# Weight jobs 14 steps later, tiles 8 to 11 closer, part of the first group's maxima by way of ScalarE

## The chip, the cores and the metric

The kernel runs on one core of one Trainium2 chip. The metric is device time in microseconds; a run ends when the output is written. Engines are named PE (TensorE, matmuls), DVE (VectorE), ACT (ScalarE), POOL (GpSimd) and SP (SyncE, which here only issues DMAs).

## The reference, cut to what is computed

x is 4 x 512 x 512, the context 4 x 1601 x 512, 16 heads of 32 columns; keys and values are both the context as it is. The hidden width of the gated block is 1408.

```python
x = x + tanh(g_xattn[0]) * mha(layernorm(x), ctx, ctx)
x = x + tanh(g_ffn[0]) * ffn(layernorm(x), w_gate, w_up, w_down, ...)
...
scores = einsum('bhqd,bhkd->bhqk', qh, kh) / sqrt(hd)
scores = where(ki <= qi + (Sk - Sq), scores, -10000.0)
out = softmax(scores) @ vh
...
qx, sx, sc = reorder_quantize(x, up_reorder_index)    # rows scaled, rounded to fp8
g, u = qlinear(qx, w_gate), qlinear(qx, w_up)          # weight rows quantized too
t = silu(g) * u
y = qlinear(reorder_quantize(t, down_reorder_index), w_down)
```

## The kernel before

**Attention.** The work is cut into 16 groups (`GALL`) of one batch and four heads. A group has 26 steps (`STEPS`): two head pairs times 13 key tiles of 128 (the last has 65). In a step PE makes the scores of two heads against one key tile (`scores`, L842 and the mask at L848), ACT takes the exponential (`exps`, L632), and PE, two steps later, multiplies by the values (`values`, L866). A score needs the stacked keys and queries `kst`, `qst`, which are 12 DMA copies for each head pair of a group (`put_heads`, L335 and L336), and a row of shifts, the negated maximum of each query, which is one DMA copy of `mrow` (`put_shift`, L340).

**Maxima.** For the shift, PE makes the same products once more from f16 halves (`max_turn`, L780, mask L785), and DVE reduces them out of PSUM (`max_reduce`, L1069). A group has 26 such chunks, two heads times up to 512 keys each; 18 of the 26 are full, and 16 of these have no mask and lie in the first 1024 keys. `max_finish` (L1076 to L1080) joins them, `shift_turn` (L794) transposes, ACT copies to `mrow` (L608). Products and reductions alternate between two slots of PSUM (`numbered`, `free_slot`). In the loop one chunk is done in a step, six steps (`AHEAD`) ahead of its group.

**Order before the loop.** PE, DVE and ACT do: the gates (L928), the stage of group 0 (transposes of keys and x, L767 and L759, split into f16 high and low parts, L592 and L1060), its 26 maxima, the shift, the stage of group 1, and six maxima of group 1. SP issues x, the keys of groups 0 and 1, three value tiles (`load_values`, L321), the 24 head copies of group 0, ten value tiles, the shift row of group 0, two blocks of w_down, the keys of group 2 and the heads of group 1.

**Feed-forward.** 26 weight jobs quantize and turn the weights: jobs 0 to 3 are blocks of w_down (128 x 1408, seven steps apart), 4 to 25 are gathered rows of w_gate and w_up (128 x 512, three steps apart). A job takes its scale on DVE (L999), is scaled by ACT (L562), rounded on DVE (L981, L985, L989), subtracted on POOL (`weight_quant`, L416, semaphore `wq_ready`) and transposed on PE (`weight_turn`, L920). With base b, a w_down job adds on DVE in step b+4, subtracts on POOL in step b+5, and turns on PE in step b+6. Then 16 tiles of 128 rows go through the block, each a chain of 27 steps over all engines (rows turn L874 at 5, up turns L887 at 7, 9, 11 and 13, hidden turn L898 at 23, down turn L910 at 25). Tiles 12 to 15 run after the last scores, which are step 415.

**What sets the order.** Every engine has one program, written step by step, and does it strictly in that order; semaphores tie the engines together. SP's program has no steps: it is one list for each group, and an issue that waits holds back all behind it. The lines of it that matter, at group 0 of the loop (`load_down(sp, o)` waits for `wq_ready` of o - 1 for o >= 2):

```python
                if gg == 0:
                    load_down(sp, 2)
                    load_down(sp, 3)
...
                if gg + 3 < GALL:
                    load_keys(sp, gg + 3)
...
                    put_heads(sp, gg + 2, 0)
...
                    put_shift(sp, gg + 1)
```

Of the kernel before, what the change touches and what calls it, by code (L numbers as in the profile page):

```python
# [5 lines left out]
def flamingo_gated_block(nc, x_d, ctx_d, gx_d, gf_d, wg_d, wu_d, wd_d, didx_d, out_d):  # L6
    nc.disable_value_cache = True
    f32, f16, bf16, i32 = mybir.dt.float32, mybir.dt.float16, mybir.dt.bfloat16, mybir.dt.int32
    ALU = mybir.AluOpType
# [51 lines left out]
    CH = len(chunks)  # L61
    assert CH == STEPS
# [3 lines left out]
    def max_job_at(at):  # L66

        gg, j = divmod(at + AHEAD, STEPS)
        return (gg + 1, j) if gg + 1 < GALL else None
# [12 lines left out]
    def tile_base(n):  # L82

        return STEPS * (n + NG) + 15 if n < TAIL else LAST + 7 + 13 * (n - TAIL)
# [18 lines left out]
    def weight_base(j):  # L103
        return 1 + 7 * j if j < DC else 1 + 7 * DC + 3 * (j - DC)
# [11 lines left out]
    banks, before_in_bank, latest, dve_count, act_count = {}, {}, {}, {}, {}  # L116

    def numbered(*job):
# [13 lines left out]
    for j in range(CH):  # L132
        numbered("max", 0, j)
# [3 lines left out]
    for j in range(AHEAD):  # L137
        numbered("max", 1, j)
    for at in range(END):
# [7 lines left out]
        if max_job_at(at) is not None:  # L147
            numbered("max", *max_job_at(at))
# [15 lines left out]
    with ExitStack() as ctx:  # L164
# [67 lines left out]

        def tile_set(n):
# [47 lines left out]
        mx_mm, m_ready, mT_mm = sem("mx_mm"), sem("m_ready"), sem("mT_mm")  # L281
        mrow_in = [sem("mrow_in0"), sem("mrow_in1")]
# [65 lines left out]
        def _(sp):  # L348
# [6 lines left out]
            for t in range(3):  # L355
# [4 lines left out]
            for t in range(3, NT):  # L360
                load_values(sp, 0, t)
# [131 lines left out]
        def _(pool):  # L493
# [91 lines left out]
        def stage_high(act, gg, part):  # L585
# [6 lines left out]
            nc.scalar.copy(to[:, gg % 2, c0:c1], slot(("stage", gg, part))[:, 0:c1 - c0]).then_inc(hi_done, 1)  # L592

# [96 lines left out]
        def _(act):  # L690
            act.wait_ge(consts, 15)
            act.wait_ge(gate_mm, 1)
            nc.scalar.activation(tg[:, :], ps[:, 0, 0:2], ACT.Tanh).then_inc(gate_th, 1)
# [3 lines left out]
            stage_high(act, 0, 0)  # L697
            norm_cols(act, 1, range(QT))
# [71 lines left out]
        def max_turn(pe, gg, j):  # L770
# [3 lines left out]
            if j == 0:  # L774
# [12 lines left out]
            last.then_inc(mx_mm, 1)  # L787

# [490 lines left out]
```

## Time and profile before

| | us |
|---|---|
| median of three runs | 1158.43 (1156.97 to 1160.3) |
| the profiled execution | 1161.19, its span 1159.4 |
| PE, DVE busy | 970.5 (84%), 859.7 (74%) |
| ACT, POOL busy | 656.5 (57%), 332.1 (29%) |
| mean granted clock of PE | 0.949 of full speed |

The durations that follow come from the one profiled execution, whose times count from the start of its span. A line of the timeline gives start, duration, engine, source line, operation, the tensors written and read, how many instructions are merged, and in brackets how long the engine had been idle and what released it. PEld is PE's weight load, SPq is SP issuing a DMA. The granted clock is a share of 2.4 GHz.

### The profile page before, as it was taken

To read this page: it belongs to the slowest core of one execution; us is meant where nothing else is said; L and a number is where in the kernel's file an instruction comes from. 1 tells how busy PE (TensorE), PEld (TensorE's weight loads), DVE (VectorE), ACT (ScalarE), POOL (GpSimd) and SP (SyncE) were. 2 spreads that over 40 slices of the span, in tenths; PEclk is the share of its full clock that TensorE was granted. 3 is DMA by queue.
4 is the path that set the end of the run, shared out by engine and by line. 5 is a ranking of instruction groups with operands and counts; after the bars stand their busy time and mean duration, and the time that the engine had idled before them with its cause. 6 is when DMAs were issued, how large, how long until landed. Compare 5 with 4: busy or idle time off the path is not lost.

```text
span 1159.4 us, 21085 instructions
## 1 busy us (share of the span) xinstructions
PE 970.5 (84%) x7770; PEld 399.4 (34%) x7770; DVE 859.7 (74%) x1438; ACT 656.5 (57%) x1343; POOL 332.1 (29%) x350
## 2 busy tenths in 40 slices
PE   4588889888879989999889999998899999984344
PEld 2233333333323334343334333333333343432222
DVE  7768789887747888777677877787778786446764
ACT  2165567675646666666556666665566666753321
POOL 3012323332101414132323232222314132443343
PEclk9998899999989999999999999999999999996766
DMA  7942423230572221114812121218421110000000
GB/s 147 154 122 69 115 66 93 66 86 26 112 88 57 66 57 39 53 43 83 124 41 60 63 61 36 51 41 115 70 61 35 27 41 10 2 10 10 10 10 19
DMA packets 155119, 70.69 MB, mean 61 GB/s; under 512 B 111032, under 2 KB 142856, under 8 KB 155016
## 3 DMA queue, kind: packets, MB, share of 16 engines
q1 hardware_dynamic: 153256, 63.57, 26.5%
q0 software_dynamic: 1760, 5.77, 1.8%
q8 instruction: 62, 1.02, 0.4%
q14 instruction: 41, 0.34, 0.1%
HBM read 39.08 MB, written 4.19 MB: 37 GB/s over the span
## 4 chain that ended last, share of the span: by engine, by line
PE 42%; DVE 36%; issue 10%; ACT 4%; POOL 4%; DMA 2%; SPq 1%; POOLq 0%; DVEq 0%; ACTq 0%
DVE mch L1069 17%; PE ps L866 13%; PE ps L842 8%; PE ps L887 6%; PE ps L780 5%; PE ps L910 3%; DVE ff L985 2%; DVE ff L981 2%; DVE ff L989 2%; PE ps L785 2%; ACT pr L632 1%; DVE upd L1112 1%; DMA qst<-mrow 1%; PE ps L848 1%; DVE cmb L1102 1%
## 5 line engine op out<-in xcount | busy, mean ns | idle before, releaser
L632 ACT ACTIVATE pr<-ps 128x512 f32<-128x512 f32 (+4 forms) x832 | 397.2, 530 | 250.0 <-PE ps L842 125.1
L1069 DVE TENSOR_REDUCE mch<-ps 128x2 f32<-128x1024 f32 (+4 forms) x416 | 432.3, 1056 | 69.2 <-PE ps L780 32.8
L866 PE MATMUL ps<-pr,vf 128*33 128x512 f32 (+4 forms) x1664 | 380.6, 537 | 0.0
L842 PE MATMUL ps<-qst,kst 97*64 97x512 f16 (+4 forms) x1600 | 250.5, 371 | 18.0 <-DMA qst<-mrow 11.4
L780 PE MATMUL ps<-kTh,qTh 32*128 32x512 f16 (+4 forms) x832 | 156.2, 373 | 59.2 <-DVE mch L1069 40.7
L780 PEld LDWEIGHTS ps<-kTh,qTh 32*128 32x128 f16 x832 | 39.5, 92 | 279.0 <-DVE mch L1069 106.9
L842 PEld LDWEIGHTS ps<-qst,kst 97*64 97x64 f16 (+1 forms) x1600 | 77.3, 111 | 108.0 <-ACT pr L632 57.4
L866 PEld LDWEIGHTS ps<-pr,vf 128*33 128x33 f32 (+1 forms) x1664 | 86.8, 113 | 56.6 <-issue 4.9
L1141 DVE SCALAR_TENSOR_TENSOR ff<-ps,scs,wsb 128x352 f32<-128x352 f32 x56 | 32.6, 583 | 73.1 <-PE ps L887 73.1
L448 POOL TENSOR_TENSOR t_q<-ff 128x768 bf16<-128x768 f32 (+1 forms) x28 | 47.4, 1694 | 100.1 <-DVE ff L989 100.1
L887 PE MATMUL ps<-wgu,t_T 128*64 128x352 bf16 x768 | 66.5, 316 | 0.0
L429 POOL TENSOR_TENSOR ff<-ff,wsb 128x352 f32<-128x352 f32 x48 | 46.0, 957 | 64.0 <-DVE ff L1141 64.0
L1060 DVE TENSOR_TENSOR kTl<-ps,kTh 128x1024 f16<-128x1024 f32 (+1 forms) x32 | 31.7, 992 | 41.0 <-ACT kTh L592 40.8
L848 PE MATMUL ps<-maskT,idb 128*64 128x128 bf16 (+2 forms) x576 | 61.7, 214 | 0.0
L989 DVE TENSOR_TENSOR ff<-ff 128x512 f32<-128x512 f32 (+3 forms) x66 | 55.0, 833 | 2.1
L659 ACT ACTIVATE ff<-ps,scs 128x352 f32<-128x352 f32 x48 | 26.6, 554 | 52.2 <-PE ps L887 52.2
L453 POOL TENSOR_TENSOR xs<-xs,ff 128x512 f32<-128x512 f32 x14 | 17.8, 1273 | 132.1 <-DVE ff L1179 132.1
L887 PEld LDWEIGHTS ps<-wgu,t_T 128*64 128x64 bf16 x768 | 44.3, 111 | 32.6 <-issue 20.8
L460 POOL TENSOR_TENSOR xs<-xs,upd 128x256 f32<-128x256 f32 x32 | 24.0, 749 | 107.9 <-DVE upd L1112 107.9
L433 POOL TENSOR_TENSOR ff<-ff 128x352 f32<-128x352 f32 x48 | 51.7, 1078 | 3.8
L489 POOL TENSOR_TENSOR cw<-w,count 128x16 f32<-128x16 f32 x16 | 3.9, 245 | 165.9 <-ACT w L615 165.9
L785 PE MATMUL ps<-idb,maskT 128*64 128x128 bf16 (+2 forms) x640 | 47.1, 229 | 0.0
(151 smaller groups left out, 1198.2 us busy)
## 6 DMA issues: line engine op xcount, KB each, us to landing
kst<-kTh SPq DMA_DIRECT2D x128, 100.1 KB, 2.2
ksrc<-in_ctx SPq DMA_DIRECT2D x16, 768.0 KB
vf<-in_ctx SPq DMA_DIRECT2D x48, 256.0 KB, 5.1
kst<-kTl SPq DMA_DIRECT2D x64, 100.1 KB, 2.2
xs<-in_x SPq DMA_DIRECT2D x16, 256.0 KB, 4.8
qst<-qTh SPq DMA_DIRECT2D x128, 32.0 KB, 1.9
out<-xs SPq DMA_DIRECT2D x16, 256.0 KB, 2.0
ff<-in_L_ffn_w_down SPq DMA_DIRECT2D x4, 704.0 KB, 4.4
```

The lines of the kernel that those rows point to most:

```text
L429: nc.gpsimd.tensor_tensor(t_u[e][:, cols], t_u[e][:, cols], wsb[:, I + c * CW:I + (c + 1) * CW], ALU.mult).then_inc(gated, 1)
L433: nc.gpsimd.tensor_tensor(t_u[e][:, cols], t_u[e][:, cols], t_g[e][:, cols], ALU.mult).then_inc(gu_ready, 1)
L448: nc.gpsimd.tensor_tensor(t_q[e][:, cols], t_v[e][:, cols], t_m[e][:, cols], ALU.subtract).then_inc(qt_ready, 1)
L632: nc.scalar.activation(pr[0:kn, n % NP, q0:S], ps[0:kn, j, q0:S], ACT.Exp, scale=SCALE).then_inc(ex_done, 1)
L780: last = nc.tensor.matmul(slot(job)[:, 512 * i:512 * i + k1 - k0], qTh[rows, gg % 2, qt * P:(qt + 1) * P], kTh[rows, gg % 2, k0:k1], start ...
L785: last = nc.tensor.matmul(slot(job)[a:e, 512 * i + lo - k0:512 * i + hi - k0], maskT[:, a:e], idb[:, lo - d0:hi - d0], start=False, stop=True)
L842: last = nc.tensor.matmul(ps[a:e, j, q0:S], kst[s][0:ST, r, k0 + a:k0 + e], qst[s][0:ST, r, q0:S], start=True, stop=(t < DT))
L848: last = nc.tensor.matmul(ps[a:e, j, q0:q0 + n_m], idb[:, a:e], maskT[:, m0:m0 + n_m], start=False, stop=True)
L866: nc.tensor.matmul(ps[64 * j:64 * j + VW, 2 + pp % 2, q0:S], vf[0:kn, t, h, :], pr[0:kn, n % NP, q0:S], start=(t == 0), stop=(t == NT - 1) ...
L887: last = nc.tensor.matmul(ps[a:e, bank(job) + side, 0:CW], qxT[:, k, a:e], wgu[:, k, side * I + c * CW:side * I + (c + 1) * CW], start=(k ...
L989: return nc.vector.tensor_tensor(v, v, m, ALU.add)
L1069: nc.vector.tensor_reduce(mch[:, qt, 2 * hp:2 * hp + 2, c], both[:, :, 0:k1 - k0], AX.X, ALU.max).then_inc(dve_free, 1)
```

## The change

- The base of weight job j moves from 1 + 7j (then 29 + 3(j - 4)) to 14 steps later. SP's list is not changed with it, apart from the loads named below.
- Tiles 8 to 11 start at steps 325, 347, 369 and 391; before it was 327, 353, 379 and 405.
- Group 0: of its 26 chunks the ten with c >= 2 (`DIRECT`) stay as they are. The 16 full chunks of the first 1024 keys (`PLAIN`, eight pairs) are made in the four PSUM banks that scores and values use later (`plain_turn`), copied by ACT to f16 buffers (`plain_copy`), and each pair is folded on DVE by three elementwise maxima and one reduction (`plain_max`).
- The first six maxima of group 1 move from before the loop into its steps 0 to 5, which then have two chunks each.
- SP issues all 13 value tiles of batch 0 ahead of the 24 head copies of group 0. The list of the loop stays.
- The gates' matmul comes after two parts of the stage; the memset of a row of `kst[1]` goes from DVE to POOL, and both such memsets go behind `row_std`.

```diff
+    PLAIN = [(hp, qt) for hp in range(PAIRS) for qt in range(QT)]
+    DIRECT = [j for j in range(CH) if chunks[j][2] >= 2]
     assert CH == STEPS
 
     AHEAD = 6
 
-    def max_job_at(at):
+    def max_jobs_at(at):
 
         gg, j = divmod(at + AHEAD, STEPS)
-        return (gg + 1, j) if gg + 1 < GALL else None
+        early = [(1, at)] if at < AHEAD else []
+        return early + ([(gg + 1, j)] if gg + 1 < GALL else [])
...
-        return STEPS * (n + NG) + 15 if n < TAIL else LAST + 7 + 13 * (n - TAIL)
+        if n < TAIL - QT:
+            return STEPS * (n + NG) + 15
+        return STEPS * (TAIL - QT + NG) + 13 + 22 * (n - TAIL + QT) if n < TAIL else LAST + 7 + 13 * (n - TAIL)
...
-        return 1 + 7 * j if j < DC else 1 + 7 * DC + 3 * (j - DC)
+        return 15 + (7 * j if j < DC else 7 * DC + 3 * (j - DC))
...
+        if job[0] == "max":
+            mx_count[job] = len(mx_count) + 1
...
+        plain = [pr[:, i, :].bitcast(f16) for i in range(NP)]
...
-            for t in range(3):
+            for t in range(NT):
                 load_values(sp, 0, t)
             sp.wait_ge(dve_free, dve_count["stage", 0, 0])
             for i in range(PAIRS):
                 put_heads(sp, 0, i)
-            for t in range(3, NT):
-                load_values(sp, 0, t)
             put_shift(sp, 0)
...
-            nc.gpsimd.memset(kst[0][ST - 1:ST, :, :], 1.0).then_inc(ones_in[0], 1)
-            pool.wait_ge(ones_in[0], 1)
             row_std(pool, 0)
+            pool.wait_ge(rstd_ready, 1)
+            for i in range(2):
+                nc.gpsimd.memset(kst[i][ST - 1:ST, :, :], 1.0).then_inc(ones_in[i], 1)
+            for i in range(2):
+                pool.wait_ge(ones_in[i], 1)
             masked_count(pool, 0)
...
+        def plain_copy(act, m, c):
+            n = 2 * m + c
+            act.wait_ge(plain_mm, n + 1)
+            if n >= NP:
+                act.wait_ge(plain_used, (n - NP) // 2 + 1)
+            nc.scalar.copy(plain[n % NP], ps[:, 2 * (n % 2):2 * (n % 2) + 2, :].rearrange("p a b -> p (a b)")).then_inc(plain_copied, 1)
...
-            act.wait_ge(gate_mm, 1)
-            nc.scalar.activation(tg[:, :], ps[:, 0, 0:2], ACT.Tanh).then_inc(gate_th, 1)
             stage_high(act, 0, 1)
             norm_cols(act, 0, range(QT))
             stage_high(act, 0, 2)
             stage_high(act, 0, 0)
+            act.wait_ge(gate_mm, 1)
+            nc.scalar.activation(tg[:, :], ps[:, 0, 0:2], ACT.Tanh).then_inc(gate_th, 1)
+            for m in range(len(PLAIN)):
+                plain_copy(act, m, 0)
+                plain_copy(act, m, 1)
             norm_cols(act, 1, range(QT))
             shift_copy(act, 0)
             masked_weight(act, 0)
...
-            if j == 0:
+            if j == 0 or (gg, j) == (0, DIRECT[0]):
...
+        def plain_turn(pe, m, c):
+            hp, qt = PLAIN[m]
+            n = 2 * m + c
+            if n >= 2:
+                pe.wait_ge(plain_copied, n - 1)
+            elif n == 0:
+                pe.wait_ge(gate_th, 1)
+            else:
+                pe.wait_ge(ps_clear, 1)
+            if n == 0:
+                pe.wait_ge(hi_done, 3)
+            for i in range(2):
+                rows = slice(HD * (2 * hp + i), HD * (2 * hp + i + 1))
+                last = nc.tensor.matmul(ps[:, 2 * (n % 2) + i, :], qTh[rows, 0, qt * P:(qt + 1) * P],
+                                        kTh[rows, 0, 512 * c:512 * c + 512], start=True, stop=True)
+            last.then_inc(plain_mm, 1)
...
+            stage_turn(pe, 0, PARTS[0])
+            stage_turn(pe, 0, PARTS[1])
             pe.wait_ge(gin, 32)
             nc.tensor.matmul(ps[:, 0, 0:2], onesf[0:1, :], gates[0:1, :], start=True, stop=True).then_inc(gate_mm, 1)
-            for part in PARTS:
-                stage_turn(pe, 0, part)
-            for j in range(CH):
-                max_turn(pe, 0, j)
+            stage_turn(pe, 0, PARTS[2])
+            for m in range(len(DIRECT)):
+                if m < len(PLAIN):
+                    plain_turn(pe, m, 0)
+                    plain_turn(pe, m, 1)
+                max_turn(pe, 0, DIRECT[m])
             shift_turn(pe, 0)
             for part in PARTS:
                 stage_turn(pe, 1, part)
-            for j in range(AHEAD):
-                max_turn(pe, 1, j)
-            pe.wait_ge(gate_th, 1)
             for at in range(END):
...
+        def plain_max(dve, s, m):
+
+            hp, qt = PLAIN[m]
+            n = 2 * m
+            a = plain[n % NP].rearrange("p (h k) -> p h k", h=2)
+            b = plain[(n + 1) % NP].rearrange("p (h k) -> p h k", h=2)
+            dve.wait_ge(plain_copied, n + 2)
+            s.step(nc.vector.tensor_tensor(a, a, b, ALU.max))
+            s.settle()
+            s.step(nc.vector.tensor_tensor(b[:, :, 0:256], a[:, :, 0:256], a[:, :, 256:512], ALU.max))
+            s.settle()
+            s.step(nc.vector.tensor_tensor(a[:, :, 0:128], b[:, :, 0:128], b[:, :, 128:256], ALU.max))
+            s.settle()
+            nc.vector.tensor_reduce(mch[:, qt, 2 * hp:2 * hp + 2, 0], a[:, :, 0:128], AX.X, ALU.max).then_inc(plain_used, 1)
...
-            dve.wait_ge(dve_free, dve_count["max", gg, CH - 1])
+            dve.wait_ge(dve_free, dve_count["max", gg, CH - 1 if gg else DIRECT[-1]])
+            if gg == 0:
+                dve.wait_ge(plain_used, len(PLAIN))
...
-            nc.vector.memset(kst[1][ST - 1:ST, :, :], 1.0).then_inc(ones_in[1], 1)
...
-                max_reduce(dve, 0, j)
+            for m in range(len(DIRECT)):
+                max_reduce(dve, 0, DIRECT[m])
+                if m < len(PLAIN):
+                    plain_max(dve, s, m)
...
-                max_reduce(dve, 1, j)
             dve.wait_ge(gate_th, 1)
...
-                if max_job_at(at) is not None:
-                    max_reduce(dve, *max_job_at(at))
+                for job in max_jobs_at(at):
+                    max_reduce(dve, *job)
```

## Rows read from the trace of the kernel before

**Rows 1.** The page's first line: the profiled execution.
```profile
span 1159.4 us, 21085 instructions
```

**Rows 2.** Stretch, us; busy us (count) of PE, PEld, DVE, ACT, POOL; granted clock; DMA share; GB/s.
```profile
700.00:760.00 60.00, 56.74 (x478) 22.99 (x476) 47.02 (x77) 38.46 (x79) 16.84 (x19) 1.00 0.18 47
```

**Rows 3.** Timeline before the loop and first scores: start us, us, engine, line, [idle before].
```profile
10.04 0.55 PE L928 MATMUL ps<-gates,onesf 1*128 1x2 f32 x2 [10.04 <-DMA gates<-in_g_ffn]
...
17.73 6.09 DVE L1069 TENSOR_REDUCE mch<-ps 128x2 f32<-128x1024 f32 x6
...
46.07 0.58 PE L794 MATMUL ps<-idh,m 128*4 128x128 f16 x4 [2.17 <-DVE m L1080]
...
53.46 6.09 DVE L1069 TENSOR_REDUCE mch<-ps 128x2 f32<-128x1024 f32 x6
...
59.82 1.06 PE L842 MATMUL ps<-qst,kst 97*64 97x512 f16 x4
```

**Rows 4.** Timeline, SyncE's queue before the loop.
```profile
14.68 5.09 SPq L321 DMA_DIRECT2D vf<-in_ctx  x3
...
52.75 0.67 SPq L340 DMA_DIRECT2D qst<-mrow  x1
```

**Rows 5.** Groups by line and shape, 0 to 70 us: count | busy us, mean ns | idle.
```profile
L1069 DVE TENSOR_REDUCE mch<-ps 128x2 f32<-128x1024 f32 x26 | 30.1, 1218 | 2.4 <-PE ps L780 2.2
...
L1060 DVE TENSOR_TENSOR kTl<-ps,kTh 128x1024 f16<-128x1024 f32 x2 | 2.5, 1226 | 3.9 <-ACT kTh L592 3.9
...
L592 ACT CAST kTh<-ps 128x1024 f16<-128x1024 f32 x2 | 2.0, 1014 | 1.5 <-PE ps L767 1.5
```

**Rows 6.** Page, DMA issues: count, KB each, median us from issue to landing.
```profile
kst<-kTh SPq DMA_DIRECT2D x128, 100.1 KB, 2.2
```

**Rows 7.** Timeline, SyncE and PE, step 104: a wait for the shift row.
```profile
319.53 1.54 SPq L340 DMA_DIRECT2D qst<-mrow  x1
...
323.77 1.07 PE L842 MATMUL ps<-qst,kst 97*64 97x512 f16 x4 [5.66 <-DMA qst<-mrow]
```

**Rows 8.** Timeline, PE only, steps 7 to 18: first weight turn, then scores of steps.
```profile
75.90 0.83 PE L920 MATMUL ps<-idb,t_q 128*128 128x128 bf16 x11 [1.65 <-POOL t_q L416]
...
91.88 0.60 PE L842 MATMUL ps<-qst,kst 97*64 97x512 f16 x4
...
104.64 0.62 PE L842 MATMUL ps<-qst,kst 97*64 97x512 f16 x4
...
106.37 0.80 PE L842 MATMUL ps<-qst,kst 97*64 97x512 f16 x4
```

**Rows 9.** Stretch as in Rows 2, from the second weight turn on.
```profile
96.00:104.00 8.00, 7.65 (x35) 3.09 (x36) 4.29 (x5) 4.39 (x10) 0.20 (x1) 0.57 0.65 193
```

**Rows 10.** Timeline, steps 15 to 29: SyncE, PE, DVE, GpSimd.
```profile
97.08 0.76 SPq L312 DMA_DIRECT2D ksrc<-in_ctx  x1
...
110.30 0.54 SPq L335 DMA_DIRECT2D kst<-kTh  x1
...
117.79 0.59 SPq L336 DMA_DIRECT2D qst<-qTl  x1
...
129.03 0.60 PE L842 MATMUL ps<-qst,kst 97*64 97x512 f16 x4
...
129.99 1.61 DVE L989 TENSOR_TENSOR ff<-ff 128x1408 f32<-128x1408 f32 x1
...
131.68 3.16 POOL L416 TENSOR_TENSOR t_T<-ff 128x1408 bf16<-128x1408 f32 x1 [5.70 <-DVE ff L989]
...
134.98 0.83 PE L920 MATMUL ps<-idb,t_T 128*128 128x128 bf16 x11 [2.02 <-POOL t_T L416]
```

**Rows 11.** Timeline, the last tiles: tile 12's statistics, tile 11's down turn, an up turn.
```profile
1053.76 0.68 DVE L1122 TENSOR_REDUCE scs<-vf 128x1 f32<-128x512 f32 x1
...
1061.89 4.33 PE L910 MATMUL ps<-wdn,t_T 128*64 128x512 bf16 x22
...
1066.06 6.13 PE L887 MATMUL ps<-wgu,vf 128*64 128x352 bf16 x80
```

More of the change, by code:

```diff
@@ L112, in turned_at @@
         return pp - 1 if rest == 0 and 1 <= pp <= GALL * PAIRS else None
-    banks, before_in_bank, latest, dve_count, act_count = {}, {}, {}, {}, {}
+    banks, before_in_bank, latest, dve_count, act_count, mx_count = {}, {}, {}, {}, {}, {}
     def numbered(*job):
@@ L131, in flamingo_gated_block @@
         numbered("stage", 0, part)
-    for j in range(CH):
+    for j in DIRECT:
         numbered("max", 0, j)
@@ L136, in flamingo_gated_block @@
         numbered("stage", 1, part)
-    for j in range(AHEAD):
-        numbered("max", 1, j)
     for at in range(END):
@@ L146, in flamingo_gated_block @@
             numbered("suf", gg)
-        if max_job_at(at) is not None:
-            numbered("max", *max_job_at(at))
+        for job in max_jobs_at(at):
+            numbered("max", *job)
         if gg + 1 < GALL and u == MT_AT:
@@ L281, in flamingo_gated_block @@
         mx_mm, m_ready, mT_mm = sem("mx_mm"), sem("m_ready"), sem("mT_mm")
+        plain_mm, plain_copied, plain_used = sem("plain_mm"), sem("plain_copied"), sem("plain_used")
         mrow_in = [sem("mrow_in0"), sem("mrow_in1")]
@@ L926, in _ @@
             pe.wait_ge(consts, 15)
+            stage_turn(pe, 0, PARTS[0])
+            stage_turn(pe, 0, PARTS[1])
             pe.wait_ge(gin, 32)
             nc.tensor.matmul(ps[:, 0, 0:2], onesf[0:1, :], gates[0:1, :], start=True, stop=True).then_inc(gate_mm, 1)
-            for part in PARTS:
-                stage_turn(pe, 0, part)
-            for j in range(CH):
-                max_turn(pe, 0, j)
+            stage_turn(pe, 0, PARTS[2])
[4 more added lines that the diff above has]
+                max_turn(pe, 0, DIRECT[m])
             shift_turn(pe, 0)
@@ L935, in _ @@
                 stage_turn(pe, 1, part)
-            for j in range(AHEAD):
-                max_turn(pe, 1, j)
-            pe.wait_ge(gate_th, 1)
             for at in range(END):
@@ L946, in _ @@
                     suffix_turn(pe, gg)
-                if max_job_at(at) is not None:
-                    max_turn(pe, *max_job_at(at))
+                for job in max_jobs_at(at):
+                    max_turn(pe, *job)
                 if gg + 1 < GALL and u == MT_AT:
@@ L1064, in max_reduce @@
             hp, qt, c, k0, k1 = chunks[j]
-            dve.wait_ge(mx_mm, gg * CH + j + 1)
+            dve.wait_ge(mx_mm, mx_count["max", gg, j])
             if gg >= 1 and j == 0:
@@ L1193, in _ @@
                 stage_low(dve, 0, part)
-            for j in range(CH):
-                max_reduce(dve, 0, j)
+            for m in range(len(DIRECT)):
+                max_reduce(dve, 0, DIRECT[m])
+                if m < len(PLAIN):
+                    plain_max(dve, s, m)
             max_finish(dve, s, 0)
@@ L1198, in _ @@
                 stage_low(dve, 1, part)
-            for j in range(AHEAD):
-                max_reduce(dve, 1, j)
             dve.wait_ge(gate_th, 1)
@@ L1211, in _ @@
                     suffix_weigh(dve, gg)
-                if max_job_at(at) is not None:
-                    max_reduce(dve, *max_job_at(at))
+                for job in max_jobs_at(at):
+                    max_reduce(dve, *job)
                 if NG <= gg < GALL and gg % NG == 0:
```

## The prediction

> **What bounds the kernel now.** I read the page first: its span [rows 1], then the busy time by stretch. In the middle of the loop PE is busy 56.7 of 60 us at full clock [rows 2], so there it is PE that is bound, and only work taken off PE, or waits of PE, count. The two ends are different. Before the loop the timeline [rows 3] shows VectorE reducing maxima almost without a gap from 17.73 us; the shift turn of group 0 waits for it until 46.07, six maxima of group 1 follow at 53.46, and the first scores start at 59.82. Beside it SyncE issues without a pause: 13 value loads and 24 head copies between 14.68 and 52.75, and only then the copy of the shift row that the first scores need [rows 4]. After the loop PE waits for chains of single tiles. The profiled execution took 1161.2 us with a span of 1159.4; the median of the runs is 1158.4. I work in span and carry the difference over to the median.
>
> **First part, before the loop.** Sixteen of 26 maxima of group 0 leave the direct route. All 26 and the finish take 46.07 - 17.73 = 28.3 us; the sixteen full ones are 16 x 1.218 = 19.5 [rows 5], so the ten that stay take about 8. In their place stand eight chains of three elementwise maxima (1024, 512 and 256 columns) and one reduction of 256, on f16 in SBUF. No row shows that form. At the rate of the nearest two-input row, 1.226 us for 1024 columns [rows 5], 2048 columns are 2.45, with about 0.2 for the small steps 2.65; at half that rate for the elementwise part 1.6. Eight are 21 or 13 us, and VectorE ends near 47.5 or 39.5. ScalarE's 16 copies at 1.014 [rows 5] are 16.2 us and lie under it. The stage of group 1 between the shift turn and 53.46 takes 7.4 us more [rows 3], so by the compute engines the first scores could start at 56 or at 48. The trace decides for f32 only.
>
> The Trainium skill, in "VectorE: DVE Perf Modes", section "What auto-detection actually checks", says that a two-input elementwise operation on 16-bit data with unit steps runs at two elements a cycle; no row of this trace has such an operation. By it the compute chain ends at 48 and has no say; without it the first scores would come about 1 us later than I take below.
>
> SyncE does not get less to do: the value loads only move ahead of the head copies, and the same 37 issues precede the shift row. PE no longer waits for the gates until 10.04 [rows 3], which frees the keys' buffer, and with it SyncE, at most 1.5 us sooner. So the shift row goes out at 51.5 to 52.7 and lands 2.2 us (the median of the head copies) to 4.2 us later [rows 6, 7]. I take the first scores at 54.8, between 53.7 and 57: 5.0 us less. The kst memset on GpSimd (before on VectorE) lies under this, as do the copies.
>
> Steps 0 to 5 now hold two maxima each. VectorE needs about 12.8 us for twelve (6.4 for the six that moved, from 53.46 to 59.82, and as much again) where six undisturbed steps of 1.73 (the distance of the last two of [rows 8]) take 10.4: +2.4, between 0 and +6.4. PE has by then been idle for some microseconds and starts at 1.2 GHz; the stretch around such a start has a mean granted clock of about 0.57 over 8 us [rows 9], a loss of about 3.4 where PE is the bound. Here VectorE paces, so +1. Together the part gives -5.0 + 3.4 = -1.6.
>
> **Second part, the weight jobs.** Jobs 0 and 1 leave steps 1 to 14. The first cost PE 1.65 of waiting and about 1.3 of work [rows 8]. From step 13 at 91.88 to step 17 at 104.64 are 12.76 us [rows 8], where four steps of 1.73 and an output turn of 0.5 make 7.4; the rest, 5.3, is job 1 with its half clock. So -8.2. All 26 jobs are still done: two w_down jobs now fall at steps 35 and 42, at 2.02 + 1.3 = 3.3 each by job 3 [rows 10], +6.6, and five gather jobs move from steps 33 to 45 to steps 98 to 110, which I take as even. Net -2; bounds -8 (all covered) and +6 (the new place collides with the batch change, where PE waits already, 5.66 us [rows 7]).
>
> **Third part, the wait this creates.** SyncE's program is in order, and its list for group 0 is: w_down block 2 (waits for quantized job 0), w_down block 3 (waits for quantized job 1), keys of group 3, twelve head copies of group 2, then the shift row of group 1. That shift row is what the scores of step 26 wait for. Before, job 1 was quantized at step 13. Now it is quantized at step 27, after the step that needs what is queued behind it. It is no deadlock: GpSimd's step 27 needs only VectorE's step 26, and this only PE's maximum, which PE issues ahead of the scores. It is a stall of PE. Its length follows from job 3, which sits in the trace at the place that job 1 gets. Step 26's scores started at 129.03; the addition ran from 129.99, GpSimd's subtraction from 131.68 for 3.16, to 134.84 [rows 10]: 5.8 after. Then w_down 0.4 and keys about 1.2 (its second issue 0.76) [rows 10]: 7.4. Twelve head copies from 110.30 to 118.38 are 8.1 [rows 10]: 15.5. The shift row then needs 2.2 to 4.2 until PE goes on [rows 6, 7]; I take 3.0: 18.5. PE resumes at half clock, +3.3 [rows 9], and the wait of 2.02 for job 3's successor in that place is gone because its data are long ready: +19.8 in all, between 15.7 and 23. Who stands behind the wait: on SyncE everything above, on PE the scores and all later steps, and through them the exponentials, the maxima and GpSimd; nothing else can run ahead.
>
> The Trainium skill, in "DMA: Bandwidth & Descriptors", section "Queues, rings and completion order", says that descriptors of one issuing queue are taken in ring order on each DMA engine. By it the shift row also stands behind the data issued just before it.
>
> **Fourth part, the tiles.** Tile 11 now ends at step 417 and not 431. Of its PE work, one up turn of 1.36, the hidden turn of about 1.3 and the down turn of 2.4 (at full clock) move into the PE-bound loop: +5.1. In the tail, VectorE's join no longer waits for a hidden chunk (2.3), and its rounding of tile 11 (5.4) no longer stands before tile 12's statistics at 1053.76 [rows 11]; the down turn (4.33 from 1061.89 [rows 11]) no longer stands before tile 12's first up turn at 1066.06: -12.0. That up turn then starts at half clock without a down turn that warms PE up: +2. Net -5; bounds -8 and -1. The loop's other engines have room: VectorE is busy 47 of 60 us [rows 2], and 22 steps instead of 26 a tile adds some 2 us to each group.
>
> **Sum.** -1.6 - 2 + 19.8 - 5 = +11.2: span 1170.6, profiled execution 1172.4, median 1169.6. I say 1169.5.
>
> **The rivals.**
> First, the same stall but dearer (16%). Behind the block 0.7 MB of weights, 0.8 MB of keys and 0.8 MB of heads leave at once; at the 193 GB/s at which the same weights and keys went in before [rows 9] they take 12 us from 6 us after the step, and the row behind them lands up to 2.2 later, at 20.2 and not 18.5: +1.7. With the weight jobs of steps 97 to 110 colliding with the batch change (+5) this gives 1176. For it: the wait at 323.77 is of that kind. Against it: heads land within 2.2 in the median [rows 6]. By the skill's rule just named it is this one, in its first half; without the rule the stall ends as summed.
> Second, the change does not do what it says before the loop (12%): the copies or the loads ahead of the heads delay the first scores to where they were, 59.8. Then +5: 1174.5. For it: SyncE is as busy as before, and 13 value loads back to back saturate the DMA engines. Against it: the count of issues is the same.
> Third, the stall pays for itself (6%), the one on the other side. While PE waits, VectorE, ScalarE and GpSimd work off weight jobs, and later steps run at 1.73 and not above 2.3. It decides if these engines can get more than about six steps ahead of PE; then up to 19 comes back: 1151. Against it: each has its own program order, with a maximum or an exponential of PE in every step.
> My forecast, the sum, has 66%; its own range is 1162 to 1177. With parts of the rivals the range is 1160.5 to 1178. A measurement of this kernel can tell about 0.3%, 3.5 us, from no change. Faster by more: 7% (the third rival and a little). Within: 7% (the forecast's low end, with all other parts at their best). Slower: 86%.
>
> **What would show it.** A wait of PE's scores for qst<-mrow of 15 to 21 us, at about 119 us from the start, with SyncE idle on GpSimd's subtraction before it and the head copies in it. First scores at 53.7 to 57 us. No PE wait for weight turns before step 21, the first at 21. Tile 12's first up turn directly behind its rows turn and no down turn of tile 11 in the tail; from the last values to the end 12 us less than before, 5 of them lost in the loop. I am wrong if that first wait is under 10 us, if the first scores start after 58, or if the steps 97 to 110 stretch by more than 6 us.

## The result and the profile after

The changed kernel takes 1185.8 us (1182.3 to 1189.3), the kernel before beside it 1157.7: ratio 1.0241, 95% interval 1.0196 to 1.0286, 27.9 us slower. The forecast was 1169.5 with a range to 1178.0: the sign was right, the size wrong by 16. The profiled execution took 1188.7 us. Below, a difference in us is the ratio of a run to the kernel before on the same chip, less one, times the latter's median.

The page of the changed kernel, its first line and the group of the scores, and below it that group on the page of before. The kernel before had 18.0 us of idle time ahead of its scores, 11.4 of them for the shift row; here it is 38.4 and 30.3.

```profile
span 1187.0 us, 21131 instructions
...
L878 PE MATMUL ps<-qst,kst 97*64 97x512 f16 (+4 forms) x1600 | 255.2, 376 | 38.4 <-DMA qst<-mrow 30.3
```
```profile
L842 PE MATMUL ps<-qst,kst 97*64 97x512 f16 (+4 forms) x1600 | 250.5, 371 | 18.0 <-DMA qst<-mrow 11.4
```

**Where the time went.** In every group ScalarE copies the shift row for the next group in step 23, which gives one mark every 26 steps. First the timeline of before, ScalarE, at steps 23, 49 and 309, then that of after at the same steps:

```profile
124.91 0.56 ACT L608 COPY mrow<-ps 4x512 f16<-4x512 f16 x1
...
189.63 0.56 ACT L608 COPY mrow<-ps 4x512 f16<-4x512 f16 x1
...
804.64 0.56 ACT L608 COPY mrow<-ps 4x512 f16<-4x512 f16 x1
```
```profile
111.89 0.56 ACT L624 COPY mrow<-ps 4x512 f16<-4x512 f16 x1
...
201.21 0.56 ACT L624 COPY mrow<-ps 4x512 f16<-4x512 f16 x1
...
818.61 0.56 ACT L624 COPY mrow<-ps 4x512 f16<-4x512 f16 x1
```

Then the busy time by stretch, columns as in [rows 2]: from step 335 to the last values, and from there to the end; before, after.

```profile
872.58:1036.33 163.75, 158.12 (x1343) 65.77 (x1342) 105.75 (x189) 108.69 (x228) 54.03 (x58) 1.00 0.08 21
1036.33:1159.40 123.07, 51.06 (x465) 30.27 (x459) 78.39 (x155) 34.55 (x54) 50.59 (x42) 0.69 0.03 11
```
```profile
888.69:1073.30 184.61, 167.37 (x1376) 68.71 (x1375) 120.27 (x206) 112.08 (x234) 60.35 (x62) 0.97 0.07 19
1073.30:1187.00 113.70, 47.28 (x414) 27.59 (x410) 68.01 (x137) 29.75 (x46) 42.03 (x35) 0.69 0.03 12
```

| after minus before, us | forecast's steps, added up | measured |
|---|---|---|
| step 23 | -1.6 - 8.2 = -9.8 | -13.0 |
| step 49 | + 19.8 + 6.6 = +16.6 | +11.6 |
| step 309 | +16.6 | +14.0 |
| last values | + 5.1 = +21.7 | +37.0 |
| end | - 12 + 2 = +11.7 | +27.6 |

At step 309 the sum is off by 2.6 us (at step 49 by 5.0), and the tail shrinks by 9.4 where 10 were forecast. The miss lies between step 309 and the last values: +23.0 instead of +5.1. Single traces scatter: in ten traces of kernels that have the code of before up to there, the copy of step 23 lies between 122.3 and 124.9. The stretch from step 335 to the last values doesn't: it takes 163.7 us in each of seven other traces with the tiles at their old steps.

**Before the loop.** VectorE, one of the new chains, then PE's shift turn, SyncE's shift row and PE's first scores:

```profile
20.46 0.68 DVE L1115 TENSOR_TENSOR pr<-pr 128x1024 f16<-128x1024 f16 x1
21.18 0.42 DVE L1117 TENSOR_TENSOR pr<-pr 128x512 f16<-128x512 f16 x1
21.63 0.29 DVE L1119 TENSOR_TENSOR pr<-pr 128x256 f16<-128x256 f16 x1
21.96 0.42 DVE L1121 TENSOR_REDUCE mch<-pr 128x2 f32<-128x256 f16 x1
...
42.10 0.58 PE L830 MATMUL ps<-idh,m 128*4 128x128 f16 x4 [3.07 <-DVE m L1134]
...
53.08 0.67 SPq L348 DMA_DIRECT2D qst<-mrow  x1
...
54.89 1.06 PE L878 MATMUL ps<-qst,kst 97*64 97x512 f16 x4 [5.21 <-DMA qst<-mrow]
```

The four instructions of a chain take 1.81 us, not 2.65: the elementwise maximum of 1024 f16 columns in SBUF is 0.68 where the two-input operation of [rows 5], which reads f32 from PSUM, is 1.23. The Trainium skill, in "VectorE: DVE Perf Modes", section "What auto-detection actually checks", gives such operations on 16-bit data the faster mode, and the trace agrees. It did not matter, as forecast: the shift turn is 4.0 us earlier than in [rows 3], and then PE waits 5.21 us for SyncE, whose list is as long as in [rows 4]. The scores start at 54.89; forecast 54.8. Steps 0 to 5, with two maxima each, take 14.0 us by ScalarE's exponentials (before 11.0, in other traces of that code up to 12.2): +3.0 at most, where +3.4 was forecast.

**Step 26.** GpSimd's subtraction of job 1, then SyncE, then PE's scores:

```profile
118.65 3.15 POOL L422 TENSOR_TENSOR t_T<-ff 128x1408 bf16<-128x1408 f32 x1 [5.70 <-DVE ff L1026]
...
121.83 0.33 SPq L334 DMA_DIRECT2D ff<-in_L_ffn_w_down  x1
...
123.56 0.53 SPq L343 DMA_DIRECT2D kst<-kTh  x1
...
131.13 0.64 SPq L348 DMA_DIRECT2D qst<-mrow  x1
...
132.91 1.06 PE L878 MATMUL ps<-qst,kst 97*64 97x512 f16 x4 [16.74 <-DMA qst<-mrow]
```

The wait is the forecast's, part by part. It begins at 132.91 - 16.74 = 116.17. The subtraction ends at 121.80, 5.6 later (forecast 5.8). Weights and keys take 1.8 until 123.56 (1.6). Twelve head copies take 7.6 (8.1). The row lands 1.8 after its issue (3.0). The granted clock was at the lower level from 117.5 to 141.4, so 8.5 us of work after the wait went at 1.2 GHz, a loss of about 4.2 (3.3).

### The profile page after: what moved, and what is told of

It reads as the page before. It is cut to its first block, busy times and chain, and to the rows that moved or that the text cites. A ratio compares the mean times of both kernels' runs of the same rounds, so it can differ in the third digit from the quotient of the medians.

```text
span 1187.0 us, 21131 instructions
## 1 busy us (share of the span) xinstructions
PE 982.0 (83%) x7770; PEld 402.6 (34%) x7770; DVE 856.2 (72%) x1453; ACT 671.1 (57%) x1359; POOL 337.3 (28%) x351
## 4 chain that ended last, share of the span: by engine, by line
PE 42%; DVE 35%; issue 9%; ACT 5%; POOL 4%; SPq 2%; DMA 2%; DVEq 0%; POOLq 0%; ACTq 0%
DVE mch L1106 14%; PE ps L902 13%; PE ps L878 8%; PE ps L923 6%; PE ps L799 5%; PE ps L946 3%; DVE ff L1022 2%; DVE ff L1018 2%; DVE ff L1026 2%; PE ps L804 2%; ACT pr L648 1%; DMA qst<-mrow 1%; DVE upd L1166 1%; DVE wsc L1036 1%; PE ps L884 1%
## 5 line engine op out<-in xcount | busy, mean ns | idle before, releaser
L1106 DVE TENSOR_REDUCE mch<-ps 128x2 f32<-128x1024 f32 (+4 forms) x400 | 414.7, 1048 | 86.8 <-PE ps L804 45.6
L902 PE MATMUL ps<-pr,vf 128*33 128x512 f32 (+4 forms) x1664 | 386.2, 544 | 0.0
L878 PE MATMUL ps<-qst,kst 97*64 97x512 f16 (+4 forms) x1600 | 255.2, 376 | 38.4 <-DMA qst<-mrow 30.3
L799 PE MATMUL ps<-kTh,qTh 32*128 32x512 f16 (+3 forms) x800 | 147.2, 366 | 57.4 <-DVE mch L1106 37.5
```

The costliest lines, as they stand in the source:

```text
L799: last = nc.tensor.matmul(slot(job)[:, 512 * i:512 * i + k1 - k0], qTh[rows, gg % 2, qt * P:(qt + 1) * P], kTh[rows, gg % 2, k0:k1], start ...
L878: last = nc.tensor.matmul(ps[a:e, j, q0:S], kst[s][0:ST, r, k0 + a:k0 + e], qst[s][0:ST, r, q0:S], start=True, stop=(t < DT))
L902: nc.tensor.matmul(ps[64 * j:64 * j + VW, 2 + pp % 2, q0:S], vf[0:kn, t, h, :], pr[0:kn, n % NP, q0:S], start=(t == 0), stop=(t == NT - 1) ...
L1106: nc.vector.tensor_reduce(mch[:, qt, 2 * hp:2 * hp + 2, c], both[:, :, 0:k1 - k0], AX.X, ALU.max).then_inc(dve_free, 1)
```

## Experiments on the wait

**One part alone: the weight jobs later, all else as before.**

```diff
-        return 1 + 7 * j if j < DC else 1 + 7 * DC + 3 * (j - DC)
+        return 15 + (7 * j if j < DC else 7 * DC + 3 * (j - DC))
```

> The kernel before with the weight jobs 14 steps later and nothing else of the change. Theory (SyncE's list): the scores of step 26 wait 15 to 19 us for the shift row behind the two w_down loads, PE then runs some 7 us at half clock; jobs 0 and 1 leave steps 1 to 14 (-8 to -9). In the changed kernel the shift copies of groups 0 to 4 show -9 up to step 23 (without the earlier start), then +24.6, +3.2 and -3.1. So +12 to +18 us, 1170 to 1176. Rival (the stall comes from the start of the changed kernel, whose SyncE work is reordered): no wait above 6 us at step 26 and -5 to +3 us.

Measured: 1.0128 (1.0089 to 1.0166), +14.9 us, with a wait of 16.73 us for the shift row at 136.39.

**The same, and SyncE's list mended.** The weight loads go behind the shift row of group 1, so that what waits for a quantized job holds back nothing that is urgent.

```diff
-                if gg == 0:
-                    load_down(sp, 2)
-                    load_down(sp, 3)
...
                     put_shift(sp, gg + 1)
+                if gg == 0:
+                    load_down(sp, 2)
+                    load_down(sp, 3)
```

> As e1_weights, and the loads of w_down blocks 2 and 3 stand in SyncE's list behind the shift row of group 1 instead of at the head of group 0. Theory (the list): the wait of step 26 goes to under 3 us, and the time falls by 16 to 21 us against e1_weights, to 1151 to 1158. Rival (the weight jobs themselves collide in their new place): it falls by less than 8 us against e1_weights.

Measured: 0.9954 (0.9934 to 0.9975), -5.3 us. The shift row is issued at 115.37, and PE does not wait in step 26. The difference to the run above is 20.2 us, by the two intervals some 15 to 25: that is the price of the created wait with its half clock (forecast 19.8). What is left, -5.3, is what it brings to do the weight jobs later (forecast -2, bounds -8 and +6).

**Does data in the queue count?** The weight jobs later, and in the list of group 0 the shift row ahead of the twelve head copies, behind weights and keys.

```diff
+                    if gg == 0:
+                        put_shift(sp, 1)
                     put_heads(sp, gg + 2, 0)
...
-                if gg + 1 < GALL:
+                if 0 < gg < GALL - 1:
                     put_shift(sp, gg + 1)
```

> As e1_weights (weight jobs later, SyncE's list as it was), with the shift row of group 1 issued ahead of the twelve head copies and not behind them. Theory (the length of the stall is the sum of the issues queued behind the block): the wait at step 26 falls from 16.7 by the twelve issues, 7.6 us, to 8 to 10 us, and the time by about 8 against e1_weights, to 1166 to 1170. Rival (data in the rings, 0.7 MB of weights and 0.8 MB of keys, decide when the row lands): the wait stays above 12 us.

Measured: 1.0095 (1.0061 to 1.0129), +11.0. SyncE's row and PE's scores:

```profile
126.74 0.65 SPq L340 DMA_DIRECT2D qst<-mrow  x1
...
132.02 1.06 PE L844 MATMUL ps<-qst,kst 97*64 97x512 f16 x4 [12.69 <-DMA qst<-mrow]
```

Counted from the start of the wait, the issue came 7.5 us sooner than in the first run, the scores only 4.0. The row needed 5.3 us to let PE go on instead of 1.8. Between them lie 0.7 MB of weights and 0.8 MB of keys issued just before. The section "Queues, rings and completion order" of "DMA: Bandwidth & Descriptors" of the Trainium skill would have the row stand behind those descriptors. This run agrees, though it doesn't tell that order from a mere sharing of the DMA engines. So the first rival named a real cost. In the changed kernel it is hidden: the 7.6 us of head issues give the data time to go, and taking them away uncovers it.

**The start alone** (the changed kernel with weight jobs and tiles at their old steps).

> The changed kernel with weight jobs and tiles where they were before: only the start is changed (maxima by way of ScalarE, value loads ahead of heads, six maxima in steps 0 to 5). Theory (SyncE's list sets the first scores at 54.9 instead of 59.8, and steps 0 to 5 give back 2 to 4): -1 to -4 us, 1154 to 1157. Rival (the gain is taken back in the loop by the weight jobs of steps 1 to 14, which now meet two maxima in a step): 0 to +5.

Measured: 0.9994 (0.9970 to 1.0019), -0.7 us; forecast -1.6, which the interval doesn't exclude. Against before it is 3.7 us ahead at step 2 and 0.7 behind at step 15: here weight jobs 0 and 1 still stand in steps 1 to 14, beside the doubled maxima. In the changed kernel, where they are gone, the same start is worth more: its step 23 comes 3.0 us sooner than in the run with the weight jobs alone, by ScalarE's exponentials at 108.2 against 111.2.

## Experiments on the tiles

**The tiles alone: 22 steps apart, all else as before** (`tile_base` as in the change, its steps 325, 347, 369, 391 instead of 327, 353, 379, 405).

> The kernel before with tiles 8 to 11 spaced 22 steps and nothing else. Theory (the loop pays): the last value product comes 20 to 23 us later and the tail is 9 to 10 us shorter, so +10 to +14 us, 1168 to 1172. Rival (my forecast's sum, the loss in the changed kernel belongs to other parts): last value +5, tail -10, so -5 us, 1150 to 1156.

Measured: 1.0109 (1.0080 to 1.0138), +12.6 us, where -5 was forecast. The three parts measured alone give 14.9 + 12.6 - 0.7 = 26.8, the whole change 27.9: they add, and the miss is this part. By stretch, the same two as above:

```profile
872.70:1056.40 183.70, 166.07 (x1376) 68.47 (x1376) 120.30 (x206) 111.99 (x234) 60.25 (x62) 0.98 0.07 19
1056.40:1170.40 114.00, 47.45 (x414) 28.05 (x410) 68.06 (x137) 29.73 (x46) 42.04 (x35) 0.68 0.03 12
```

From step 335 to the last values it is 20.0 us longer than before: 8.0 more busy time of PE, of which some 3 are half clock and 5 the work that moved in (as forecast), and 12.0 more idle time, which was forecast at nothing. In the tail 9.1 come back. PE's waits in the first stretch (what, released by: us in total, times, longest), tiles alone and then before:

```profile
PE ps L782 <- DVE mch L1071: 4.8, 5, 2.5
PE ps L876 <- POOL t_q L425: 3.9, 2, 2.2
PE ps L844 <- ACT pr L634: 2.8, 6, 0.6
PE ps L782 <- DVE kTl L1062: 1.8, 1, 1.8
```
```profile
PE ps L780 <- DVE mch L1069: 1.8, 2, 1.0
PE ps L842 <- ACT pr L632: 1.4, 2, 0.8
```

VectorE is busy 120 of 184 us here. So my argument, that the other engines have room, looked at a sum, and I tried moves to see what it hides.

**All four two steps earlier, at the old distance of 26** (325, 351, 377, 403).

> The kernel before with tiles 8 to 11 at steps 325, 351, 377 and 403, two steps earlier with the spacing of 26. Theory (places count, and tile 11's rounding must stay behind the join of step 420): up turns at places 20, 22, 24 and 0 keep two of four in the light steps, and the rounding comes at steps 421 and 422, behind the join but in part ahead of the last statistics: +1 to +6 us. Rival (only the spacing matters): -2 to +1.

Measured: 1.0084 (1.0057 to 1.0111), +9.7, more than expected. The four stand as far apart as before, and yet the stretch to the last values takes 8.5 us more (172.2), with the tail as it was: where in the 26 steps a tile's pieces fall counts by itself.

**One distance of 22, then 26** (325, 347, 373, 399).

> The kernel before with tiles 8 to 11 at steps 325, 347, 373 and 399: one spacing of 22, then 26, so that tiles 9, 10 and 11 begin at place 9 of their groups (15 before). Theory (place: up turns and statistics meet full maxima and stages): steps 335 to 361 lose 6 to 8 us and steps 361 to 387 lose 5 to 7, though the spacing is 26 there; the tail is 6 to 9 shorter; in all +6 to +10, 1164 to 1169. Rival (density): steps 361 to 387 lose nothing, in all -2 to +3.

Measured: 1.0109 (1.0062 to 1.0156), +12.6, with a wide interval. Steps 335 to 361 take 6.1 us more than before, steps 361 to 387 2.9 more, though the distance there is 26 again.

**Only tile 11, four steps earlier** (327, 353, 379, 401).

> The kernel before with only tile 11 moved, to step 401 from 405, where the loop has no maxima any more. Both theories of the tiles: steps 335 to 387 unchanged. The down turn of tile 11 then still stands at step 426, ahead of the first up turn of tile 12, but earlier work leaves the join and the statistics free: -1 to -4 us, 1155 to 1158. If it is above +2, the steps after 387 lose too and the place is not the whole cause.

Measured: 1.0059 (1.0037 to 1.0081), +6.8: slower, where both theories had it faster. Steps 335 to 387 take what they took (113.6 us), so all of it lies behind step 387: some 3 us up to the last values, the rest after them. VectorE around the last join, which the tail waits for:

```profile
1043.43 0.22 DVE L1101 TENSOR_TENSOR den<-cw,ps 128x4 f32<-128x4 f32 x2
...
1045.24 0.90 DVE L987 TENSOR_SCALAR ff<-ff 128x640 f32<-128x640 f32 x1
1046.17 2.30 DVE L991 TENSOR_TENSOR ff<-ff 128x640 f32<-128x640 f32 x1
1048.39 2.46 DVE L1019 BATCH_NORM_STATS2 stat<-xs 128x6 f32<-128x512 f32 x4
```

Half of tile 11's rounding now stands between the join and the last statistics, which are 3.7 us apart (before 1.7), and its last step takes 2.30 us beside GpSimd's subtraction of the other half, against 0.83 for the same operation in a quiet place.

**Is it the reductions?** Both kernels, before and tiles alone, with the reductions of groups 13 to 15 over 64 columns instead of up to 512. This leaves out most of the maximum of these groups, so only times are read.

```diff
-            nc.vector.tensor_reduce(mch[:, qt, 2 * hp:2 * hp + 2, c], both[:, :, 0:k1 - k0], AX.X, ALU.max).then_inc(dve_free, 1)
+            kw = 64 if gg >= 13 else k1 - k0
+            nc.vector.tensor_reduce(mch[:, qt, 2 * hp:2 * hp + 2, c], both[:, :, 0:kw], AX.X, ALU.max).then_inc(dve_free, 1)
```

> The kernel before, but VectorE reduces only 64 columns of each half of a maximum chunk for groups 13 to 15 (this leaves most of these maxima out; PE makes the products as before). It is the comparison for e11. PE is 95 to 99% busy in steps 335 to 387, so if PE is the bound there nothing changes: -3 to 0 us. If VectorE were the bound, these 52 steps would shrink by more than 8 us.

> The same with tiles 8 to 11 spaced 22 steps (e3_tiles with narrow reductions for groups 13 to 15, which leaves most of these maxima out). Theory (in the shifted places PE waits for VectorE, whose full reductions, stages and tile steps meet there): steps 335 to 387, 14 us longer than before in e3_tiles, are then 2 to 6 us longer than in e12, and the time is -4 to +3 us against e12 where e3_tiles is +12.6 against before. Rival (PE's own order or ScalarE: up turns beside full scores, whoever reduces): 10 us or more stay, and the time is +8 or more against e12.

Measured: before so cut 0.9957 (0.9939 to 0.9976), -5.0 and so more than expected; tiles alone so cut 1.0027 (1.0013 to 1.0042). The tiles still cost 8.1 us. From step 335 to the last values they still cost 17.2 of the 20.0 (178.6 against 161.4), although VectorE is now busy only 88.0 of the 178.6 us; PE waits 1.84 us for the keys' low part at 907.43 and 1.70 for the rows' halves at 965.86. So the amount of VectorE's work is a small part of it at most.

**The coincidence.** In the tiles-alone run the wait for the keys' low part and the two for the rows' halves have one picture. VectorE and GpSimd around step 350, then PE's three waits:

```profile
910.15 0.75 DVE L1181 SCALAR_TENSOR_TENSOR ff<-ps,scs,wdb 128x512 f32<-128x512 f32 x1 [2.80 <-PE ps L912]
910.82 0.42 DVE L983 TENSOR_SCALAR ff<-ff 128x512 int32<-128x512 int32 x1
911.27 1.38 DVE L987 TENSOR_SCALAR ff<-ff 128x512 f32<-128x512 f32 x1
912.68 0.69 DVE L991 TENSOR_TENSOR ff<-ff 128x512 f32<-128x512 f32 x1
913.29 0.75 DVE L1062 TENSOR_TENSOR kTl<-ps,kTh 128x577 f16<-128x577 f32 x1
```
```profile
910.98 1.38 POOL L455 TENSOR_TENSOR xs<-xs,ff 128x512 f32<-128x512 f32 x1 [14.07 <-DVE ff L1181]
913.45 1.26 POOL L425 TENSOR_TENSOR t_q<-ff 128x512 bf16<-128x512 f32 x1 [1.09 <-DVE ff L991]
```
```profile
914.10 0.20 PE L782 MATMUL ps<-kTh,qTh 32*128 32x65 f16 x2 [1.84 <-DVE kTl L1062]
...
974.12 0.38 PE L876 MATMUL ps<-idb,t_q 128*128 128x128 bf16 x4 [1.72 <-POOL t_q L425]
...
1020.01 0.38 PE L876 MATMUL ps<-idb,t_q 128*128 128x128 bf16 x4 [2.20 <-POOL t_q L425]
```

A tile takes its down result (L1181) in its step 25 and rounds its rows (L983 to L991) in its step 3. With 22 steps between tiles 25 - 22 = 3: the two fall into one step, for tiles 8 and 9, 9 and 10, 10 and 11, and VectorE's program puts the down result first. VectorE idles 2.80 us for it while the rounding stands behind it (with the order changed, below, it starts at 907.52); then one of the three operations takes 1.38 us, while GpSimd adds the down result, instead of the 0.43 it has alone; then the keys' low part and the halves are late. The section "SBUF: two separate sides" of "SBUF — State Buffer" of the Trainium skill says that GpSimd and those VectorE operations that use a second port take a shared pair of ports in turn, each for a whole instruction; the trace agrees, since the operation ends 0.3 us after GpSimd's. The test keeps the 22 steps and changes the order in the step alone: VectorE rounds first, and GpSimd makes the halves in that step, ahead of its addition.

```diff
                 for n, k in tiles_at(at):
-                    if k == 4:
+                    if k == 3 and n < TAIL:
+                        round_rows(pool, n)
+                for n, k in tiles_at(at):
+                    if k == 4 and n >= TAIL:
                         round_rows(pool, n)
...
                 for n, k in tiles_at(at):
+                    if k == 3:
+                        rows_round(dve, s, n)
+                for n, k in tiles_at(at):
                     if k == 1:
                         rows_stats(dve, s, n)
-                    if k == 3:
-                        rows_round(dve, s, n)
```

> The kernel before with tiles 8 to 11 spaced 22 steps (as e3_tiles, which was 12 us slower than before), and in addition: where the down result of one tile (step 25 of the tile) and the rounding of the next tile's rows (its step 3) fall into the same step, VectorE rounds the rows first and takes the down result after, and GpSimd makes the halves of the rows in that step too, ahead of its addition of the down result. Theory of coinciding steps: with 22 steps the two fall together for tiles 8 and 9, 9 and 10, 10 and 11 (25 - 22 = 3), the rounding stands behind the down result that VectorE waits for, one of its three operations takes 1.38 us instead of 0.42 beside GpSimd's addition, and TensorE waits 1.84 us for the keys' low part, 1.72 and 2.20 us for the halves, with a stretch of half clock behind the first. With the order changed these three waits fall to under 0.5 us each and the run is 4 to 7 us faster than e3_tiles: +5 to +9 against before. Rival (VectorE has simply too much work for 22 steps, whatever its order): the waits go to the next maxima, and it stays within 2 us of e3_tiles, +10 to +13.

Measured: 1.0023 (1.0003 to 1.0043), +2.7 us instead of +12.6, and better than expected. PE's longest waits and the two stretches:

```profile
PE ps L785 <- DVE mch L1074: 4.3, 4, 2.5
PE ps L847 <- ACT pr L637: 2.8, 6, 0.6
PE ps L813 <- DVE mch L1074: 0.7, 1, 0.7
PE ps L903 <- DVE kTl L1065: 0.7, 1, 0.7
```
```profile
872.95:1050.15 177.20, 165.68 (x1376) 68.30 (x1375) 118.04 (x206) 111.93 (x234) 59.93 (x62) 0.98 0.08 20
1050.15:1159.50 109.35, 46.15 (x414) 27.80 (x410) 70.04 (x137) 29.50 (x46) 42.33 (x35) 0.69 0.03 13
```

The three waits, 5.8 us, are gone, and the first stretch is 6.5 us shorter. VectorE's order and GpSimd's were changed together and not tested apart. The tail is 4.7 shorter too, since the order also acts there. How much of the gain that is, the order alone with the old tiles tells:

> The kernel before with the rounding order alone. By the first reading the whole gain lies behind the last value: 3 to 5 us faster than before, the loop unchanged within 1 us. By the rival: within 1 us of before.

Measured: 0.9965 (0.9945 to 0.9985), -4.1 us.

```profile
1038.83:1158.60 119.77, 51.08 (x465) 30.52 (x459) 80.41 (x155) 34.35 (x54) 50.95 (x42) 0.69 0.03 12
```

The loop is unchanged (163.7 us from step 335 to the last values). From there to the end it takes 119.8 instead of 123.1; PE's waits for the rows of tiles 14 and 15 there fall from 13.59 and 12.34 us to 11.98 and 10.74. So of the 9.9 us, about 4 are the tail and about 6 the coincidence in the loop.

**The 2.50 us wait that is left,** at tile 9's two hidden roundings: tile 9 one step earlier (325, 346, 369, 391), with the new order.

> As e14_round_first, and tile 9 starts at step 346 instead of 347 (tiles 325, 346, 369, 391), nothing else. In e3_tiles TensorE waited 2.50 us for a maximum at 953.0, because the two roundings of tile 9's hidden rows (0.56 + 0.56 + 0.96 and 1.20 + 0.49 + 0.83 us) stand in steps 365 and 366, between maxima of 1024 columns of 1.22 us each and ahead of the join of step 368; half a clock of 3 us followed. One step earlier the first of them stands beside a maximum of 642 columns (about 0.5 us). Theory of the place: that wait falls to under 1.5 us and the half clock goes: 2 to 4 us faster than e14_round_first. Rival (only the number of steps counts): within 1 us of e14_round_first.

Measured: 1.0018 (0.9997 to 1.0040). The longest wait for a maximum falls to 1.0 us, and in the traces the time at the lower clock in the loop falls from some 6.8 to 3.4 us and the stretch to the last values by 2.1, to 175.1. But the tail is 1.0 longer, the waits for exponentials rise from 2.8 to 3.4, and the ratios differ by 0.6 us only, which their intervals can't tell from nothing or from 2. The theory's step held; a gain in the whole time isn't shown.

## Putting it together

All of the change with SyncE's list mended:

> The whole change with only SyncE's list corrected (w_down loads 2 and 3 behind the shift row of group 1). Theory (costs add): the stall and its half clock go, -20 us against the changed kernel as in e2 against e1; what is left is start -0.7, weight jobs -5, tiles +12.6, so +6 to +8 against before, 1164 to 1168. Rival (the tiles' loss in the changed kernel comes from being later after the stall): below +2.

Measured: 1.0078 (1.0051 to 1.0105), +9.0; the parts measured alone add up to +6.6. Mended, with the new order and tile 9 at 346:

> The changed kernel with SyncE's list mended (w_down 2 and 3 behind the shift row of group 1, as e5_after_list, which was 9.5 us slower than before), the rounding order of e14_round_first and tile 9 at 346. If the three causes add, it gains on e5_after_list what e15_round_first_346 gains on e3_tiles, some 6 to 10 us: within 3 us of before. Rival: the clock and the waits elsewhere give it back, and it stays at +6 to +9.

Measured: 0.9958 (0.9940 to 0.9977), -4.9, better than expected. In its trace no half clock is left between step 335 and the last values (granted clock 1.00), and the stretch still takes 11.3 us more than before, 175.1: 5.2 more busy time of PE, the work that moved in, and 6.1 more idle time. Mended, and the tiles at their old steps:

> The changed kernel with two corrections: the w_down loads 2 and 3 behind the shift row in SyncE's list, and the tiles where they were before. Theory (the parts add): the start -0.7, the weight jobs with the corrected list -5.2, together -6 us, 1151 to 1155. With the first scores at 54.9 and no weight job in steps 0 to 5 it may reach -8. Rival (the two gains are the same one, PE time ahead of step 14): -3 to -5.

Measured: 0.9960 (0.9936 to 0.9984), -4.6, where -6 was expected. The same with the new order:

> The changed kernel with SyncE's list mended and tiles 8 to 11 at their old steps (the kernel of e7_best, 4.6 us faster than before), and with the rounding of the rows ahead of the other tile work of a step on VectorE, as in e14_round_first. With the old tiles no down result falls into the step of a rounding inside the loop, but in the tail the order applies to tiles 14 and 15: there e14_round_first needed 109.4 us from the last value to the end where e3_tiles needed 114.0. If that gain of 4.6 us belongs to the order and not to the 22 steps, this is 3 to 5 us faster than e7_best: 8 to 10 us faster than before. Rival (the tail is paced by tile 12, which the order doesn't reach): within 1 us of e7_best.

Measured: 1150.2 us, 0.9909 (0.9886 to 0.9932), -10.5. This is the fastest of the runs, faster than both kernels: the early loads and copies of the change, its later weight jobs, the mended list, the old tiles, the rounding first.

## Why the prediction was right and wrong

- **What bounds.** Right for the loop and the ends, and too coarse for the fourth part (below). Of the three signs by which the forecast called itself wrong none came: the wait was 16.74, the first scores 54.89, and steps 75 to 127, where the last weight jobs now stand, took 124.0 us (before 127.2). None of them watched the tiles.
- **First part.** Forecast -1.6, alone -0.7. First scores 54.8 and 54.89. That SyncE and not VectorE sets them was right; the chains at 1.81 us lie between the two sizes that were worked out, 2.65 and 1.6, nearer to the lower, and this changed nothing.
- **Second part.** Forecast -2, measured -5.3, inside its bounds. The clearest term sized too small is the first one: from the exponentials of step 6 to the copy of step 23 pass 42.3 us instead of 53.4, where -8.2 was forecast. How much too small stays open, since the code of before takes 50.9 to 53.4 there in other traces.
- **Third part.** Right in mechanism, place and size: wait 16.74 (18.5), with half clock 20.2 (19.8) within some 5. Landing and head copies were shorter than taken, the half clock dearer.
- **Fourth part.** This is the part that failed: net -5 was forecast, with bounds of -8 and -1, and the tiles alone cost +12.6. The tail was right (-9.4 against -10): tile 12's first up turn starts 12.4 us sooner after the last values (forecast 12.0) and then takes 7.69 us for 6.13, at half clock (+2). Right too were the 5 us of moved PE work. Wrong was the step "The loop's other engines have room: VectorE is busy 47 of 60 us", which put the loop's new waits at nothing; they are 12.0 us, with some 3 of half clock. It asks for an average. What counts is which pieces fall into the same step of an in-order program: down result and rounding, because 25 - 22 = 3. The runs show 6 us for this one coincidence in the loop. The rest, 8.5 us beyond the moved work with the order mended, is waits for maxima (4.3 us, before 1.8) and for exponentials (2.8, before 1.4), other short waits, and half clock. Which moved piece causes which of them stays open.
- **Rivals.** None named the tiles. The dearer stall was a real mechanism but a covered one, and the collision at the batch change that it also named didn't come (steps 75 to 127, above). The start did what it says. The stall did not pay for itself: between steps 49 and 309 nothing of it came back.
- **The range** took its upper end from the stall alone. The fourth part had bounds of -8 and -1 with no end on the other side, though the trace of before did not show four tiles at that distance.

## What to carry to other kernels

Before moving a piece of a chain that repeats every N steps, take its offsets modulo N and list what now shares a step on each in-order engine; if a piece that waits stands ahead of one that is ready, swap them. And before delaying a producer, read what is queued behind its consumer, on the DMA-issuing engine too. A busy share tells neither.

## What the runs showed of the hardware

- VectorE's operation on 512 f32 columns with one input took 0.43 us alone and 1.38 beside an addition on GpSimd; one with two inputs and 640 columns 0.83 and 2.30, beside GpSimd's subtraction of 2.04. In these steps the two engines together were dearer than their parts.
- A copy of one small row needed 1.8 us from issue to use behind head copies, and 5.3 behind 1.5 MB issued in the microseconds before it.
- After a wait of 16.7 us the clock stayed at 1.2 GHz for 8.5 us of work. Waits as short as 1.84 and 2.50 us in the loop (914.1 and 953.0, tiles alone) were each followed by 3.4 us at the lower level, 916.2 to 919.6 and 953.8 to 957.1, so each cost some 1.7 us more than its length. But it need not be so: the waits of 1.72 and 2.20 us at 974.1 and 1020.0 of the same run were followed by full clock.
